# Relu layer of a two-layer attention and expert network: ScalarE writes the normalised rows, VectorE applies scale and residual in two wide passes one step later, GpSimd's bias addition is issued before its square root

## The reference, cut to what matters

```
def _layernorm(x, gamma, beta):
    mean = jnp.mean(x, axis=-1, keepdims=True)
    std = jnp.sqrt(jnp.mean((x - mean) ** 2, axis=-1, keepdims=True))
    return (x - mean) / (std + EPS) * gamma + beta
...
h = relu(x @ ff_w1 + ff_b1) @ ff_w2 + ff_b2       # 128 -> 512 -> 128
x = residual + layernorm(h + y, g3, b3)
```

## Time and profile before

| what | value |
|---|---|
| median of three runs | 2000.6 us (1999.92 to 2000.62) |
| the profiled execution | 2002.31 us |
| its span in the profile | 2000.5 us |
| mean granted TensorE clock | 0.957 |
| busy: PE / DVE / ACT / POOL | 1794.0 / 1487.9 / 977.3 / 617.3 us |
| the relu layer, from its first sum on VectorE to the first product of the shared experts | 1299.97 to 1474.14 us |

### The profile page before, as it was taken

The page is one execution under the profiler, slowest core; times in us unless marked ns, Lnnn a source line. Parts: engine busy times, 40 slices in busy tenths (PEclk is TensorE's granted clock), DMA queues, the critical chain, the costliest instruction groups (busy, mean ns, idle before and its releaser), DMA issues. The chain is left out here.

```text
span 2000.5 us, 48705 instructions
## 1 busy us (share of the span) xinstructions
PE 1794.0 (90%) x18012; PEld 1367.1 (68%) x18012; DVE 1487.9 (74%) x4059; ACT 977.3 (49%) x2040; POOL 617.3 (31%) x754
## 2 busy tenths in 40 slices
PE   7999998788879999999999999789959798899994
PEld 4666666577765666666666666567748677778883
DVE  5777776677745888888888888679957566667885
ACT  5566662466654555555554555255543233334341
POOL 1111010111101322332223232254755355654342
PEclk9999996899997999999999999889979899999997
DMA  3100000000000000000100010275021255566884
GB/s 145 33 21 31 21 21 1 1 1 0 1 22 1 1 0 0 0 0 1 33 22 31 21 31 10 67 275 195 32 110 42 78 190 177 192 192 201 265 274 132
DMA packets 71330, 143.66 MB, mean 72 GB/s; under 512 B 8496, under 2 KB 35504, under 8 KB 65584
## 3 DMA queue, kind: packets, MB, share of 16 engines
q1 hardware_dynamic: 60208, 122.52, 18.7%
q0 software_dynamic: 11008, 19.68, 2.7%
HBM read 94.11 MB, written 48.05 MB: 71 GB/s over the span
## 5 line engine op out<-in xcount | busy, mean ns | idle before, releaser
L530 DVE TENSOR_REDUCE mx<-ps 128x8 f32<-128x512 f32 x384 | 262.1, 683 | 160.3 <-PE ps L750 160.2
L421 ACT ACTIVATE ex<-ps 128x512 f32<-128x512 f32 x384 | 230.3, 600 | 265.4 <-PE ps L771 263.4
L771 PE MATMUL ps<-pack,sh 128*128 128x128 f32 x1536 | 252.2, 287 | 29.9 <-DVE sh L532 29.0
L532 DVE TENSOR_TENSOR sh<-ps,mx 128x512 f32<-128x512 f32 x384 | 265.5, 691 | 13.2
L1445 ACT ACTIVATE late_hT<-ps 128x512 f32<-128x512 f32 x184 | 110.3, 600 | 307.6 <-PE ps L1563 282.8
L787 PEld LDWEIGHTS ps<-vblk,ex 128*64 128x64 f32 x6144 | 214.4, 140 | 66.0 <-issue 66.0
L787 PE MATMUL ps<-vblk,ex 128*64 128x32 f32 x6144 | 257.4, 227 | 0.0
L771 PEld LDWEIGHTS ps<-pack,sh 128*128 128x128 f32 x1536 | 170.2, 143 | 122.0 <-issue 65.2
L1334 POOL DMA_INDIRECT done<-late_acc,late_to_i x152 | 147.7, 972 | 200.8 <-DVE late_acc L2015 165.9
L750 PE MATMUL ps<-kblk,qd 32*64 32x256 f32 x3072 | 207.7, 387 | 1.5 <-issue 1.5
L2015 DVE SCALAR_TENSOR_TENSOR late_acc<-ps,late_w,late_acc 128x128 f32<-128x128 f32 x456 | 128.0, 343 | 46.6 <-PE ps L1610 39.5
(11 more groups left out here) (317 smaller groups left out, 3457.5 us busy)
## 6 DMA issues: line engine op xcount, KB each, us to landing
late_wbuf<-parts SPq DMA_DIRECT2D x38, 1024.0 KB
sent<-late_rows SPq DMA_DIRECT2D x1, 12136.0 KB, 37.7
late_rows<-sent SPq DMA_DIRECT2D x38, 296.0 KB
late_down<-in_down SPq DMA_DIRECT2D x38, 256.0 KB
ctxT<-in_ctx SPq DMA_DIRECT2D x32, 256.0 KB, 2.8
sent<-late_rows SPq DMA_DIRECT2D x1, 7400.0 KB, 25.1
late_raw<-done SPq DMA_DIRECT2D x11, 512.0 KB
x_res<-in_x SPq DMA_DIRECT2D x16, 256.0 KB, 2.9
```

What stands on the lines that cost most here:

```text
L421: nc.scalar.activation(ex[:, u % 2], UB[u % 4].rearrange("p (c n) -> p c n", n=P), ACT.Exp).then_inc(e_ready, 1)
L530: nc.vector.tensor_reduce(mx[:, u % 2], sc, AX.X, ALU.max).then_inc(max_done, 1)
L532: nc.vector.tensor_tensor(sh[:, u % 4].rearrange("p (h k) -> p h k", k=S), sc, mx[:, u % 2].unsqueeze(2).broadcast_to((P, HH, S)), ALU.sub ...
L771: last = nc.tensor.transpose(UB[u % 4][:, c * P:(c + 1) * P], sh[:, u % 4, c * P:(c + 1) * P], ident)
```

## The change

ScalarE gets a new piece of work, `norm_z(g)`: four activations z = t1 * rs + ms, where ms = -mean * rs is computed by a small new operation on VectorE. VectorE's per-tile passes `zg` and `x_res` are replaced by two operations over all four tiles at once, z * g3 and z + x_res; they stand in a new function `finish(g)`, together with `norm_stats(g)`, which is called in step g + 1 between `bn_aggr` and the wait for `std_done`, and once after the last step. The routing work of a step now comes in one piece at the step's end. VectorE's sum of a step waits for `z_done` of the step before. GpSimd issues `biased_x(g + 1)` ahead of `root(g)`, with a wait for `summed`. The tile `zg` goes, the tiles `ms` and `z` come.

```diff
-        zg = sb("zg", [P, TILES, D])
+        ms = sb("ms", [P, TILES])
+        z = sb("z", [P, TILES, D])
...
             for g in range(NG):
+                if g + 1 < NG:
+
+                    pool.wait_ge(summed, nth(g))
+                    biased_x(g + 1)
                 root(g)
-                if g + 1 < NG:
-                    biased_x(g + 1)
...
+            def norm_z(g):
+                act.wait_ge(shift_done, nth(g))
+                if g >= 1:
+                    act.wait_ge(x_done, g)
+                for t in range(TILES):
+                    last = nc.scalar.activation(z[:, t, :], t1[:, t, :], ACT.Identity, bias=ms[:, t:t + 1],
+                                                scale=rs[:, t:t + 1])
+                last.then_inc(z_done, 1)
...
                 if g + 1 < NG:
                     copy_yT(g + 1)
+                if g >= 1:
+                    norm_z(g - 1)
                 if g - 1 in COUNT_AT:
                     copy_counts(COUNT_AT[g - 1])
...
+            norm_z(NG - 1)
             copy_counts(COUNT_AT[NG - 1])
...
                 dve.wait_ge(out_ready, nth(g))
+                if g >= 1:
+                    dve.wait_ge(z_done, g)
...
                 last.then_inc(r_moments, 1)
-                dve.wait_ge(r_moments, nth(g))
-                for t in range(TILES):
-                    last = V.scalar_tensor_tensor(zg[:, t, :], t1[:, t, :], r_mv[:, t, 0:1], C["g3"], ALU.subtract, ALU.mult)
-                last.then_inc(zg_done, 1)
-                if fill:
-                    route(fill[0], fill[1][:1])
+                if g >= 1:
+                    finish(g - 1)
                 dve.wait_ge(std_done, nth(g))
                 V.reciprocal(rs[:, :], se[:, :]).then_inc(r_rstd_done, 1)
                 dve.wait_ge(r_rstd_done, nth(g))
+                V.scalar_tensor_tensor(ms[:, :], r_mv[:, :, 0], -1.0, rs[:, :], ALU.mult, ALU.mult).then_inc(shift_done, 1)
+                if fill:
+                    route(*fill)
+
+            def finish(g):
+
+                dve.wait_ge(z_done, nth(g))
+                V.tensor_tensor(z[:, :, :], z[:, :, :], across(C["g3"], TILES), ALU.mult).then_inc(zg_done, 1)
                 dve.wait_ge(zg_done, nth(g))
                 dve.wait_ge(x_biased, nth(g))
-                for t in range(TILES):
-                    xt = x_res[:, g * TILES + t, :]
-                    last = V.scalar_tensor_tensor(xt, zg[:, t, :], rs[:, t:t + 1], xt, ALU.mult, ALU.add)
-                last.then_inc(x_done, 1)
+                xs = rows_of(x_res, g)
+                V.tensor_tensor(xs, z[:, :, :], xs, ALU.add).then_inc(x_done, 1)
                 norm_stats(g)
-                if fill:
-                    route(fill[0], fill[1][1:])
...
+            finish(NG - 1)
             make_table(0)
             low_rows(0)
```

More of the change, by code:

```diff
@@ L1093, in late_phase @@
         r_rstd_done = sem("r_rstd_done")
+        shift_done = sem("shift_done")
+        z_done = sem("z_done")
         zg_done = sem("zg_done")
```

## The result

The changed kernel takes 2052.35 us (median of 4, 2051.76 to 2054.69) against 2000.61; the ratio is 1.0259, with a 95% interval of 1.0239 to 1.0279. Forecast was 2059.6, with a range from 2040 to 2078. The profiled execution took 2054.69 us, its span is 2052.9.

What follows compares the result with a forecast made beforehand. VectorE's backlog at the relu layer's end was taken as the bound. Summed steps moved the first shared product from 1474.14 to 1530.4, +56 us; with 3 for TensorE's clock, 59 us more gave 2059.6 us, range 2040 to 2078.

Steps and rivals of the forecast that it cites:

- The hand-over in front of VectorE: After moments(g-1), GpSimd does norm_power, bias and root while VectorE idles 4.5 us a step, 60 to 70 in all.
- The bias under the moments: GpSimd's bias of g+1 runs under the moments of g only at g = 0; otherwise it comes behind norm_power.
- ScalarE's z: VectorE's next sum waits for ScalarE's four activations, 1.8 us with releases, hidden only in steps with routing fill.
- The two wide passes: VectorE's two whole-width operations, in place of zg and the final pass, take 0.70 us each.
- ms in steps 1 to 5: VectorE's ms waits beside GpSimd's two subtractions: 2.3 us in steps 2 to 5, 1.2 in step 1.
- TensorE just off the path, plus 3 us for its clock: TensorE's way takes 12.4 us against VectorE's 13.3 or more; 3 us added for clock falls, bounds 0 and 12.
- the price of a fall of the clock: TensorE's slower work after idling costs 1.6 to 3.1 us per fall; slack or fill takes it in most steps.
- The tail: Step 15 and the tables, with finish(15) and copy_counts, up to the first shared product: 20.5 us.
- The DMA wait under the delay: ScalarE's 9.17 us wait for a raw weight load goes under the later steps, leaving no more than a us or two.
- the 9.7 us of a step: Time from VectorE's sum to shift_done(g) in a step: 2.0 + 2.8 + 4.5 + 0.4 us.
- faster: Rival, chance 0.05: GpSimd has root(g) ready when finish(g-1) ends, the wait is covered; about 5 us less, 1995.6.

Runs made afterwards that it cites:

- e1: Changed kernel with norm_power(g-1) issued behind root(g) on GpSimd instead of ahead of the bias and root; 2001.0 us against 2001.09 of the kernel before.
- e2: Changed kernel with GpSimd's bias issued behind the root, norm_power still ahead; 2044.2 us, ratio to the kernel before 1.021.
- e7: Changed kernel with GpSimd's subtractions in steps 1 to 5 held until ms is through; 2048.38 us, ratio 1.0266.
- e5: e1 with ScalarE's copied counts ahead of norm_z in steps 9 and 13; 1996.15 us against 1996.1 of the kernel before.
- e3: Changed kernel with the whole routing fill issued ahead of the wait for std_done instead of behind it; 2043.97 us, ratio 1.0208.
- e9: Kernel before with only the SP queue's first clearing of slots moved behind the stores of split weights; 1990.16 us against 1995.44.

## Why the prediction was right, point by point

- **The hand-over in front of VectorE** was put at 4.5 us in each of the later steps, 60 to 70 us in all. The trace has 66.0 us, 4.37 in nearly every step, and e1 shows that it is the cause.
- **The bias under the moments** was forecast only for g = 0. That is how it came.
- **ScalarE's z** at 1.8 us between shift_done and the sum: 1.78 in steps 2, 4, 6 and 10, which have no fill ahead of them. In steps 3 and 5 TensorE's 2.54 and 2.25 us are later still.
- **The two wide passes** at 0.70 each: 0.66 and 0.69.
- **ms in steps 1 to 5** is the term that was mis-sized most. I took 2.3 us in steps 2 to 5, that is a wait for both of GpSimd's subtractions. `ms` took 1.00 us: it waited for the one that was running (to 1329.32) and was through at 1329.35, long before the end of the second. That is 4 x 1.5 = 6 us too much; step 1 (0.46 us) gives another 1.0. e2 shows such a wait for a single operation, the bias: 0.83 us, through 0.02 us behind it. The rule of the Trainium skill, SBUF — State Buffer, section "Who interferes with whom", that one excludes the other for a whole instruction, fits this trace; my step from one instruction to a queue of two did not follow from it. In the earlier trace rows four passes met three operations, which is one wait for each and no evidence that one pass waits for two.
- **TensorE just off the path, plus 3 us for its clock.** It was on the path ahead of four sums: the sum waits for it in 6 steps, 22.7 us together, of which 12.1 fall before the sums of steps 0 and 1 and the rest to steps 3, 5, 9 and 13. Steps 10 to 14 took from 1427.38 to 1505.54, 78.2 us where I had 75.9; step 13 has the largest of these waits, 3.58 us, behind the counts, as forecast. Steps 3 and 5, where I had the slack take the price of a fall of the clock, cost 0.8 and 0.5 us beyond the wait for z. Behind the pause in step 2 the transposition and the H products took 1.08 and 5.22 us, against 0.63 and 3.60 in the next step, with a granted clock of 0.78 over the step:

```profile
1320.71 1.08 PE L1524 MATMUL ps<-pack,rows_in 128*128 128x128 f32 x4 [5.41 <-ACT rows_in L1387]
1321.59 5.22 PE L1554 MATMUL ps<-late_yT,pack 128*128 128x512 f32 x8
```

- **The tail** was put at 20.5 us (its terms add up to 20.3) and took 19.5 (1505.54 to 1525.05).
- **The DMA wait under the delay:** 9.17 us became 5.8, at most 2.9 at a time, somewhat more than the one or two that I had. Whether part of TensorE's lateness in steps 3 and 5 comes from it was not separated; e2 and e7, where both grew, point that way.

The layer was forecast at 1530.4 + 3 - 1300.0 = 233.4 us and took 225.0. The difference of 8.4 us, stretch by stretch (forecast less measured): step 1 12.7 - 11.5, steps 2 to 5 55.2 - 49.2, steps 6 to 8 47.0 - 47.9, step 9 11.5 - 11.2, steps 10 to 14 75.9 - 78.2, the tail 20.5 - 19.5, and the 3 us that I had put down beside the steps for the clock.

The total came nearer than its terms. Too high were `ms` by 7.0 us, the 9.7 us of a step by 0.3 in 14 steps (step 6 has 9.39 from the sum to the end of `ms`) and the tail by 1.0, some 12 us together. Too low was TensorE: its waits beyond z, ahead of steps 3, 5, 9 and 13, cost 0.8 + 0.5 + 2.2 + 3.6 = 7 us where 3 stood. The two make 12 - 4 = 8 us. That errors of both signs met is luck. The hand-over itself, which by e1 is most of the slowdown, was right in its mechanism and in its size.

The rival "faster" said that 1995.6 would come if the wait for std_done were covered. e1 and e5 cover it, and the kernel is only as fast as before, not 5 us faster. The saving is real: in e5 steps 6, 7, 10, 11 and 13 are 0.7 to 0.8 us shorter than in the kernel before. But step 9 is 2.3 us longer, steps 2 and 12 are 1.0 longer and the tail 3.1. It is bought with a later start of TensorE's transpositions: the moments of step g-2, on which they hang, are now made in step g-1. TensorE waits 11.7 us in 6 steps for `rows_in` in e5, where it was 5.2 us in 4 in the kernel before. The tail is 15.9 us instead of 12.8, for finish(15). How much each of the two takes was not tried alone.

## What to carry to other kernels

When a piece of work is deferred by a step, look in every other engine's queue for what waits for its result, and move that wait too. Here VectorE deferred the moments, GpSimd kept its wait for them ahead of the root that VectorE needs next, and two in-order queues took turns; the place of one call was worth 46 us. And a wait that is taken out is not yet time that is won: ask which wait ends last behind it, and what the moved work runs into. e2 took out 14.7 us of waiting and gained 3.8: a bias in a new place held up `ms`, and in the first steps TensorE was late. In e3 the routing in its new place ran beside GpSimd's work and took longer, and the waits for TensorE and for z grew.

## What I had not expected

- VectorE gets in between two back-to-back operations of GpSimd: `ms` ended at 1329.35, 0.03 us behind the first subtraction's end, and the second took 1.27 us, as without a neighbour. The cost of a meeting is the rest of one operation, not of the queue.
- 1.05 us less of waiting a step in e2 brought 3.8 us in the layer, not 16. From step 6 on, 0.67 of each 1.05 us went into `ms`, which now met the bias; up to step 5 TensorE's pieces, stretched by 2 us behind pauses of 4.73 and 1.11 us (5.59 against 3.60, 5.97 against 3.73), took nearly all.
- The largest gain of this case lay outside the change: 12 MB of clearing that queued ahead of weight loads, 5.3 us in the medians (e9).
